# A decoder layer in fp32 on one core: GpSimd splits the values' weights early and the output's weights late in self-attention's first batch

## The reference, cut to what matters

```
x = x + self_attention(layernorm(x), w_qkv, w_out)    # 16 heads of 32, causal
x = x + cross_attention(layernorm(x), ctx, wq, wk, wv, wo)
x = x + mixture_of_experts(layernorm(x), wg, W, b)    # 8 experts, the best one of each token
```

## Time and profile before

| | us |
|---|---|
| median of 3 runs | 798.06 (796.03 to 798.13) |
| the profiled execution | 796.43 |
| its span, first to last instruction | 794.7 |
| TensorE busy in the span | 685.9 (86%) |
| VectorE busy | 503.6 (63%) |
| GpSimd busy | 312.5 (39%) |
| ScalarE busy | 308.7 (39%) |

### The profile page before, as it was taken

How to read it: one execution, slowest core, us unless ns; L and a number is a source line. 1 busy time by engine, 2 the same in 40 slices (tenths; PEclk the granted TensorE clock), 3 DMA queues, 4 the chain that set the end, 5 groups by cost and what they waited for, 6 DMA issues and landing times. The chain is left out here.

```text
span 794.7 us, 19084 instructions
## 1 busy us (share of the span) xinstructions
PE 685.9 (86%) x6040; PEld 610.3 (77%) x6041; DVE 503.6 (63%) x1456; ACT 308.7 (39%) x984; POOL 312.5 (39%) x534
## 2 busy tenths in 40 slices
PE   4569999999999996578999999999999986239995
PEld 4569898888889895477988888888889975228884
DVE  4577887878778867186645464656565557626663
ACT  3356566666656564143232232323232343102220
POOL 0556756666675756144000101010101046435662
PEclk9789999999999998679999999999999998559998
DMA  9265876656656466196212222222222046246530
GB/s 340 77 107 91 124 138 142 140 111 139 142 116 143 104 131 150 50 319 232 97 64 80 80 79 79 79 79 79 79 79 79 0 132 185 80 136 183 185 118 17
DMA packets 142885, 95.07 MB, mean 120 GB/s; under 512 B 110846, under 2 KB 115070, under 8 KB 142720
## 3 DMA queue, kind: packets, MB, share of 16 engines
q1 hardware_dynamic: 137184, 82.00, 40.0%
q0 software_dynamic: 5664, 12.61, 5.2%
HBM read 56.14 MB, written 18.77 MB: 94 GB/s over the span
## 5 line engine op out<-in xcount | busy, mean ns | idle before, releaser
L400 ACT ACTIVATE prob<-prob,shift 128x128 f32<-128x128 f32 (+1 forms) x256 | 114.6, 449 | 117.1 <-POOL shift L328 116.6
L60 PE MATMUL b_bank<-w_hi 128*128 128x256 f32 (+1 forms) x576 | 119.8, 331 | 7.3 <-DVE w_lo L1191 7.2
L1003 ACT CAST w_hi<-b_bank 128x256 fp32r<-128x256 f32 (+1 forms) x144 | 60.3, 446 | 160.6 <-PE b_bank L60 143.4
L60 PE MATMUL b_bank<-w_lo,w_hi 128*128 128x256 f32 (+1 forms) x576 | 115.2, 323 | 0.0
L60 PE MATMUL b_bank<-w_hi,w_lo 128*128 128x256 f32 (+1 forms) x576 | 114.7, 322 | 0.0
L60 PEld LDWEIGHTS b_bank<-w_hi 128*128 128x128 f32 x576 | 89.8, 195 | 16.0 <-DVE w_lo L1191 8.1
L600 DVE CUSTOM_DVE_ANT_0 prob<-a_s,mask 128x128 f32<-128x128 f32 (+1 forms) x256 | 79.6, 348 | 32.7 <-PE a_s L476 32.6
L1191 DVE TENSOR_TENSOR w_lo<-b_bank,w_hi 128x256 fp32r<-128x256 f32 (+1 forms) x144 | 68.3, 507 | 47.2 <-ACT w_hi L1003 47.1
L60 PEld LDWEIGHTS b_bank<-w_lo,w_hi 128*128 128x128 f32 x576 | 91.3, 195 | 8.1
L60 PEld LDWEIGHTS b_bank<-w_hi,w_lo 128*128 128x128 f32 x576 | 90.7, 194 | 7.6
L328 POOL TENSOR_SCALAR shift<-nmax 128x2 f32<-128x2 f32 x128 | 42.4, 332 | 105.7 <-DVE nmax L600 102.1
(11 more groups left out here) (169 smaller groups left out, 1372.1 us busy)
## 6 DMA issues: line engine op xcount, KB each, us to landing
stage<-in_w SPq DMA_DIRECT2D x8, 1024.0 KB, 5.5
xin<-in_x SPq DMA_DIRECT2D x8, 512.0 KB, 4.1
xr<-in_x SPq DMA_DIRECT2D x8, 512.0 KB, 4.1
x<-xr SPq DMA_DIRECT2D x8, 512.0 KB, 3.2
xin<-x SPq DMA_DIRECT2D x8, 512.0 KB, 4.3
b_cin_t<-in_ctx_t SPq DMA_DIRECT2D x8, 512.0 KB, 3.6
b_cin<-in_ctx SPq DMA_DIRECT2D x8, 512.0 KB, 3.5
xr<-x SPq DMA_DIRECT2D x8, 512.0 KB, 4.3
```

The lines of the kernel that those rows point to most:

```text
L60: ins = pe_matmul(out, a, b, start=first and i == 0, stop=last and i == len(steps) - 1)
L400: a = nc.scalar.activation(prob[:, e % NPROB, cols], prob[:, e % NPROB, cols], ACT.Exp, scale=-1.0, bias=shift[:, e, q:q + 1], accum_out=r ...
L1003: nc.scalar.copy(hi, src).then_inc(job_hi, 1)
```

## The change

GpSimd gets a new function, `value_weights`, which casts and subtracts a whole value half (`u`, then `w`; 4 x 256 columns on each partition) in its own queue. It runs both ahead of slot 0, behind the first `next_rstd(0)`, and waits for the load of the values' weights (`w_in[2]`). `u` and `w` leave `PIECES` and `SPLIT_LATER`, so that ScalarE and VectorE no longer split them in slots 2 and 4. The four chunks of the output's weights move from GpSimd's slots 0, 1, 2, 3 to its slots 8, 9, 12, 13 of batch 0. On TensorE the jobs `u0` and `w0` of batch 0 wait for the new semaphore `wv_split` in place of `w_split`.

```diff
--- before.py
+++ after.py
@@ -109,6 +109,7 @@
         consts, tick, tick_sp, tick_pool = sem("a_consts"), sem("a_tick"), sem("a_tick_sp"), sem("a_tick_pool")
         tick_pe = sem("a_tick_pe")
         w_split_hi, w_split, wo_hi_done, wo_split = sem("w_split_hi"), sem("w_split"), sem("wo_hi_done"), sem("wo_split")
+        wv_hi_done, wv_split = sem("wv_hi_done"), sem("wv_split")
         ln_dve, ln_rstd, xn_ready = sem("a_ln_dve"), sem("a_ln_rstd"), sem("a_xn_ready")
         job_done, job_hi, job_ev = sem("a_job_done"), sem("a_job_hi"), sem("a_job_ev")
         s_done, mx_done, shift_done, ex_done = sem("s_done"), sem("mx_done"), sem("shift_done"), sem("ex_done")
@@ -134,10 +135,10 @@
 
         PASSES = ((0, 0), (1, 0), (0, 1), (1, 1), (2, 0))
 
-        PIECES = ("q0", "k0", "q1", "k1", "q2", "k2", "q3", "k3", "u", "w")
+        PIECES = ("q0", "k0", "q1", "k1", "q2", "k2", "q3", "k3")
         SPLIT_FIRST = {"X0": ["q0"], "X1": ["k0"], "q0": ["q1"], "k0": ["k1"], "q1": ["q2"], "k1": ["k2"]}
-        SPLIT_LATER = {0: ["q3"], 1: ["k3"], 2: ["u"], 4: ["w"]}
-        WO_LATER = {0: 0, 1: 1, 2: 2, 3: 3}
+        SPLIT_LATER = {0: ["q3"], 1: ["k3"]}
+        WO_LATER = {8: 0, 9: 1, 12: 2, 13: 3}
 
         def piece_columns(piece):
             i = "qkuw".index(piece[0])
@@ -319,6 +320,14 @@
                 pool.wait_ge(wo_hi_done, c + 1)
                 nc.gpsimd.tensor_tensor(wo_lo[:, c, :], raw[:, 3, c, :], wo_hi[:, c, :].bitcast(F32),
                                         ALU.subtract).then_inc(wo_split, 1)
+
+            def value_weights(i, piece):
+                cols = piece_columns(piece)[1]
+                pool.wait_ge(w_in[2], 16)
+                nc.gpsimd.tensor_copy(w_hi[:, :, cols], raw_columns(piece)).then_inc(wv_hi_done, 1)
+                pool.wait_ge(wv_hi_done, i + 1)
+                nc.gpsimd.tensor_tensor(w_lo[:, :, cols], raw_columns(piece), w_hi[:, :, cols].bitcast(F32),
+                                        ALU.subtract).then_inc(wv_split, 1)
 
             def slot(n, h):
                 e = head_at(h, 0, n)
@@ -358,6 +367,8 @@
                     out_weights(WO_LATER[h])
 
             next_rstd(0)
+            for i, piece in enumerate("uw"):
+                value_weights(i, piece)
             for h in range(H):
                 slot(0, h)
             with pool.Fori(1, B - 1) as n:
@@ -440,8 +451,10 @@
                     pe.wait_ge(job_ev, job_at("X1", n) + 1)
                 if j == "y0":
                     pe.wait_ge(ot_hi_done, n * G)
-                if isinstance(n, int) and n <= 0 and j[0] in "qkuw" and not (n == 0 and j in NEXT):
-                    pe.wait_ge(w_split, PIECES.index(j if j in PIECES else j[0]) + 1)
+                if isinstance(n, int) and n <= 0 and j[0] in "qk" and not (n == 0 and j in NEXT):
+                    pe.wait_ge(w_split, PIECES.index(j) + 1)
+                if isinstance(n, int) and n == 0 and j in ("u0", "w0"):
+                    pe.wait_ge(wv_split, "uw".index(j[0]) + 1)
                 if last_in_bank(j, n):
                     pe.wait_ge(job_ev, job_at(*last_in_bank(j, n)) + 1)
                 if j[0] == "X":
```

## The result

The changed kernel took 790.93 us (median of 4, 790.19 to 792.9) beside 797.12 for the kernel before (4 runs): ratio 0.9928, 95% interval 0.9902 to 0.9954. So the change wins about 6 us (6.2, 6.3, 5.7). The forecast was 2.4 and the range ended at 793.2: the prediction was wrong in the size of the gain. The first changed execution that was profiled took 792.90 us (span 791.1, clock 0.935), 3.5 less than the profiled one of before, and is the slowest of these four. Two more profiles of the same kernel (e1: 787.92, e13: 789.91) are needed to read it.

The account below looks back on a forecast made before the run. Batch 0 was taken as bound by the ring VectorE, GpSimd, ScalarE and its weight splits. Prologue +1.1, slots 0 and 1 -1.1, `u` -3.5, `w` -3.8 less 1.3, queue +3.6: 2.4 us won, 795.7 us, range 793.2 to 799.8.

Parts of the forecast that it names:

- The lock: VectorE with two SBUF inputs and GpSimd reading SBUF exclude each other; prologue 1.1 us late, some 0.4 a chunk.
- the first rival: More is won: the lock costs much less in prologue and GpSimd's queue, gain 4.1, 794.0 us; chance 0.22.
- the third rival: Slower: GpSimd's last chunk holds TensorE before batch 1 if a chunk costs 3.4 us; 800.5 us; chance 0.17.
- -3.5 for `u`: Slot 2 of batch 0: without the split of `u`, VectorE's wait of 2.06 and work of 1.49 us go.
- -3.8 for `w` less 1.3 that TensorE's order keeps: Batch 0 behind head 4's maxima: 3.8 us won without the split of `w`, 1.3 of it kept by TensorE's order.
- Shifted, I take it at 1.2 GHz to 39.3: TensorE in batch 0: half clock to 39.3, then 2.4 GHz, so group 2's scores start at 42.15, 6.0 us ahead.
- the queue from head 8's to head 14's shift: GpSimd, slots 8 to 13: about 18.1 us back to back with the four chunks, head 14's shift at 62.4.
- and the lead is kept: From `k2` of batch 1 on TensorE is saturated, so the 2.4 us won there last to the end.
- theory B: Expectation of e1: something outside batch 0 was won too, batches 1 to 7 or later parts over 0.5 us shorter.
- the second, 797.3: No change: TensorE's clock returns one step (3.4 us) later, group 2 starts at 43.8, gain 0.75; chance 0.20.

Follow-up runs that it names:

- e1: The changed kernel once more, beside the kernel before: 789.99 us, ratio 0.9914.
- e13: The changed kernel once more, on another chip: 790.67 us, ratio 0.9932.
- the filled kernels: The kernel before (794.37 us) and the changed kernel (790.22 us), each with idle products of the identity in TensorE's waits of batch 0.
- e9: The kernel before with 44 idle products of the identity in TensorE's waits of batch 0: 794.37 us, ratio 0.9959.
- e5: The kernel before with 80 idle products in batch 0, which held TensorE too long: 796.6 us, ratio 1.0003.
- e6: The changed kernel with 62 idle products in TensorE's waits of batch 0: 790.22 us, ratio 0.992.
- e15: The changed kernel with 39 idle products in batch 0, on another chip: 789.66 us, ratio 0.9916.
- e3: The kernel before with only the output's weights moved to slots 8, 9, 12, 13: 798.0 us, ratio 1.0022.
- e4: The changed kernel with zero fills, behind `next_rstd(0)`, in place of the output's weights' split: 792.2 us, ratio 0.9949.
- e8: The changed kernel with zero fills, ahead of `next_rstd(0)`, in place of the output's weights' split: 787.55 us, ratio 0.9906.
- e2: The changed kernel with the output's weights back in slots 0 to 3, so the value splits alone: 791.81 us, ratio 0.9953.
- e10: The changed kernel with 39 idle products in TensorE's waits of batch 0: 795.92 us, ratio 0.997.
- e12: The changed kernel with the output's weights' chunks in slots 0, 1, 8, 9: 796.49 us, ratio 0.9977.

## Why the prediction was wrong

**Right, by their own steps.** The order of events held throughout:

| step | forecast | after | e1 |
|---|---|---|---|
| first maxima | 21.6 | 21.20 | 21.82 |
| head 2's maxima | 29.15 | 28.59 | 29.20 |
| head 3's maxima | 31.8 | 31.14 | 31.75 |
| head 5's maxima | 36.3 | 35.52 | 35.44 |
| group 2's scores | 42.15 | 40.26 | 40.12 |
| head 8's shift | 44.3 | 43.33 | 43.25 |
| group 3's scores | 50.1 | 48.69 | 48.60 |
| last chunk done | 62.4 | 60.75 | 60.65 |
| group 0's scores, batch 1 | 62.4 | 62.02 | 61.12 |
| `k2`, batch 1 | 66.3 | 65.28 | 64.49 |

The lock is there and is priced about right: 2.39 and 2.71 us for GpSimd's wide subtractions, 2.19 for `k2`'s low half (in e1 `q2`'s), 1.45 for a chunk's subtraction. So the first rival gave the nearest number (794.0) for a reason that is not there. TensorE never waited for the last chunk, which rules out the third rival; a chunk took 0.62 + 0.08 + 1.45 = 2.15 us, not 2.95.

**The first step that failed: the sum up to group 2's scores, for which TensorE was taken at half clock to 39.3.** The forecast had these scores 6.0 us ahead (-3.5 for `u`, -3.8 for `w` less 1.3 that TensorE's order keeps); they are 7.9 ahead in the profile of after and 8.0 in e1. "Shifted, I take it at 1.2 GHz to 39.3": the clock was back at 35.6 in the profile of after, and in e1 it did not fall before 48.1. Head 5's maxima were 0.8 us early besides. But head 8's shift follows only 1.0 before its forecast, as it comes through GpSimd's values' lower parts (39.76 to 43.25, in place). Then a chunk was sized at 2.35 and took 2.15, and the queue from head 8's to head 14's shift took 17.5 in place of 18.1. So it ended at 60.84 and not 62.4. In the profile of after half clock from 59.5 to 62.9 took 0.8 of it back. The forecast gave `k2` 2.4 us; it won 3.4, 4.2 and (e13, 64.53) 4.2. By the start of batch 2 the three profiles are 3.4, 4.4 and 4.2 us ahead of 101.60, 4.0 on the mean; between the filled kernels it is 4.6 (101.90 and 97.26).

**The second: "and the lead is kept" was taken as the whole gain.** The lead was kept: from batch 2 to the last scores it is 205.07 us before, 205.23 after, 205.26 in e13, and 0.6 less in e1 (204.43). But behind that, in code that no edit touched, time goes too: 488.03 before, 487.70 after, 484.57 in e1, 485.52 in e13, 485.60 in e9. The stretch that opens it, in the kernel before (all of it, then its part at half clock) and in e1:

```profile
306.67:341.20 34.53, 16.97 (x182) 13.02 (x181) 13.46 (x39) 8.52 (x27) 9.71 (x20) 0.68 0.39 89
312.40:332.90 20.50, 11.93 (x102) 9.28 (x103) 4.81 (x13) 4.08 (x14) 4.89 (x10) 0.50 0.39 87
```

```profile
301.63:334.56 32.93, 15.57 (x182) 11.99 (x181) 13.45 (x39) 8.52 (x27) 9.72 (x20) 0.69 0.38 93
307.50:324.60 17.10, 8.87 (x95) 6.88 (x96) 4.16 (x11) 4.06 (x14) 4.80 (x9) 0.50 0.43 101
```

The same 182 products, 1.6 us less, with the return to full clock 3.4 us sooner after its fall. A median execution of before (796.4, less 1.7 around the span and 101.6) has 693.1 us behind the start of batch 2, one of the changed kernel (790.4, 1.7 and 97.6) has 691.1: the other 2 us. This 2.0 is what the 4.0 of the profiles leaves of 6.0, so it adds up by its making; but the profiles give the same (485.9 on the mean of three against 488.03). With the first step put right and this one left, the forecast would have been 798.06 - 4.0 = 794.1, inside the range, and the measured 790.93 still outside. Another 0.9 us of the distance lies in the median of before itself, 798.06 of three runs in the forecast and 797.12 of four beside the result.

That filling TensorE's waits in batch 0 shortens this part, and hardly batch 0, is shown by e9, and by e5 and the table above. For the changed kernel the clock is thus the likely cause of the 2 us, by the same pattern; one profile each and intervals of 2 us leave its size open. The whole of the half clock time doesn't tell an execution's time: twice (1 - mean clock) x span averages 101 to 102 us over the runs of before, 99.1, 93.5 and 95.5 over the three sets of the changed kernel and 89.4 in e9, but also 83.6 in e6 and 83.0 in e15, which are hardly faster than the changed kernel, 86.0 in e5 and 98.5 in e3, which win nothing. Why a fall of the clock in batch 0 should move one 250 us later is not shown. The expectation of e1 had named the sign of this (theory B: a later part shorter by over 0.5 us). That an edit changes the clock's steps was among my rivals as a loss only (the second, 797.3); no rival had it as a gain.

## What to carry to other kernels

Work moved from a chain of several engines into one engine's idle time is paid back where that engine's queue is full: sum that queue instruction by instruction (here 17.5 us against a forecast of 18.1). Where to place the displaced work is read from a marker behind both places, and not from the first engine that it blocks: the early place put group 2's scores 3.5 us late, and 0.4 of it was left at batch 2. Such a marker deep in the kernel gives the chain's gain to about 1 us from a few profiles. But where the granted clock moves between two levels, an edit can shift its steps in code far behind it, to either side: take three profiles or more of each kernel (there is one of the kernel before here), and put a term of some 2 us for the clock into the range. Filling the waits with idle products in both kernels helps to tell the chain from the clock.

## What was not expected of the hardware

- A write alone blocks too (e4): GpSimd's fills (0.51 us each, `memset` of 128x512) beside VectorE's `tensor_scalar` of 128x512 fp32 made a pair of these take 4.44 us in place of 1.00 (e8). And a `tensor_scalar` of two columns took 1.27 us in place of 0.17 behind a GpSimd subtraction (e2).
- Who comes first decides who pays, and it changes from one execution of the same kernel to the next: the same low half (`q2`) took 0.75 us in the profile of after, where it began 0.3 us before the subtraction of `w`, 2.19 in e1 and 2.20 in e13, where it began 0.7 us behind it, and 2.83 in e2.
- GpSimd pays as well: its cast of 1024 columns took 1.04 us alone and 1.52 beside VectorE's low halves, its subtraction 2.39 and 2.71.
- The waits of ScalarE and VectorE in the experts' loop of e10 to e12 (five of up to 4.6 us, released by nothing in the trace) came in most executions of three kernels on one chip, by their times (a median 6 to 7 us longer in the two that were run again), and in none of those two on another.
